# Inverse roots of a local-attention pipeline as exp(-0.5 ln x) under one activation table set, with a Newton step on GpSimd

## The reference

```python
def l2norm(t): return t / jnp.clip(jnp.linalg.norm(t, axis=-1, keepdims=True), 1e-12)

def _layer(x, wqkv, qs, ksc, wo, lg, lb, w1, b1, w2, b2):
    qkv = shift_token(x) @ wqkv                  # 8 heads of 64
    q, k, v = split_into_heads(qkv)
    q = l2norm(q) * qs;  k = l2norm(k) * ksc     # 16 norms a token
    q, k = rotary_xpos(q, k)
    x = x + local_attention(q, k, v) @ wo        # windows of 64, softmax
    h = shift_token(x)
    h = (h - h.mean(-1)) / jnp.sqrt(h.var(-1) + 1e-5) * lg + lb   # 1 norm a token
    a, g = jnp.split(h @ w1 + b1, 2, axis=-1)
    return x + (a * gelu(g)) @ w2 + b2
for l in range(2):
    x = _layer(x, ...)
```

## Time and profile before

| | |
|---|---|
| time, median of 3 runs | 1845.13 us (1841.08 to 1846.48) |
| the profiled execution | 1845.41 us, span 1843.6 us |
| local pipeline, from its first instruction to the tail's | about 1269 to 1656 us of the span |
| busy over the span: PE, DVE, ACT, POOL | 1734.1, 1442.4, 1408.9, 1431.1 us |
| mean granted TensorE clock | 0.976 of full speed |

### The profile page before, as it was taken

One profiled execution on the slowest core, in us unless ns is written; L12 is line 12 of the kernel. 1 busy time (PEld: TensorE's weight loads), 2 busy tenths in 40 slices (PEclk: granted clock), 3 DMA queues, 4 the chain that ended last, 5 costly groups with the idle time before them and its releaser, 6 DMA issues. The chain is left out here.

```text
span 1843.6 us, 54099 instructions
## 1 busy us (share of the span) xinstructions
PE 1734.1 (94%) x22920; PEld 1099.5 (60%) x22920; DVE 1442.4 (78%) x2658; ACT 1408.9 (76%) x1737; POOL 1431.1 (78%) x851
## 2 busy tenths in 40 slices
PE   5999999999999999999999999987899999978997
PEld 2466666666666666666666666675566666653454
DVE  5888888888888888888888887535888888855785
ACT  2688888888888888888888888943898888853464
POOL 6699999999999999999999999974765566634122
PEclk9899999999999999999999999998999999989999
DMA  5101010101011010101010100041111111100000
GB/s 141 27 20 31 19 31 22 28 25 29 24 27 26 25 31 19 31 23 28 23 31 19 28 20 9 2 157 29 40 41 37 37 37 37 33 25 2 1 0 23
DMA packets 71080, 57.02 MB, mean 31 GB/s; under 512 B 29196, under 2 KB 64184, under 8 KB 70840
## 3 DMA queue, kind: packets, MB, share of 16 engines
q1 hardware_dynamic: 70840, 53.57, 11.5%
HBM read 14.67 MB, written 1.05 MB: 9 GB/s over the span
## 5 line engine op out<-in xcount | busy, mean ns | idle before, releaser
L278 POOL TENSOR_TENSOR ah_probs_lo<-ah_probs,ah_probs_hi 128x1024 f16<-128x1024 f32 x512 | 1073.2, 2134 | 78.0 <-ACT ah_probs L487 77.9
L542 DVE TENSOR_REDUCE ah_part_max<-ah_p_m 128x1 f32<-128x512 f32 x1024 | 668.5, 685 | 121.5 <-PE ah_p_m L342 111.2
L484 ACT ACTIVATE ah_probs_hi<-ah_p_s 128x1024 f16<-128x1024 f32 x512 | 530.9, 1037 | 189.6 <-PE ah_p_s L358 178.4
L487 ACT ACTIVATE ah_probs<-ah_p_s 128x1024 f32<-128x1024 f32 x512 | 531.3, 1038 | 0.0
L372 PE MATMUL ah_p_o<-ah_v_hi,ah_probs_hi 128*128 128x65 f16 x4096 | 470.6, 195 | 5.7 <-POOL ah_probs_lo L278 5.1
L374 PE MATMUL ah_p_o<-ah_v_lo,ah_probs_hi 128*128 128x64 f16 x4096 | 470.6, 193 | 0.0
L376 PE MATMUL ah_p_o<-ah_v_hi,ah_probs_lo 128*128 128x65 f16 x4096 | 470.3, 194 | 0.0
L372 PEld LDWEIGHTS ah_p_o<-ah_v_hi,ah_probs_hi 128*128 128x128 f16 x4096 | 383.0, 98 | 84.4 <-DVE a_attn L565 12.2
L374 PEld LDWEIGHTS ah_p_o<-ah_v_lo,ah_probs_hi 128*128 128x128 f16 x4096 | 378.5, 98 | 91.3
L342 PE MATMUL ah_p_m<-ah_k_hi_lo,ah_q_hi_twice 128*128 128x512 f16 x1024 | 393.8, 385 | 6.6 <-DVE ah_part_max L542 3.5
L357 PE MATMUL ah_p_s<-ah_q_hi_twice,ah_k_hi_lo 128*128 128x512 f16 x1024 | 388.6, 380 | 0.8 <-ACT ah_probs L487 0.4
(11 more groups left out here) (316 smaller groups left out, 3083.4 us busy)
## 6 DMA issues: line engine op xcount, KB each, us to landing
ba_v_skew<-ba_v_own SPq DMA_DIRECT2D x64, 129.0 KB, 2.3
ah_q_hi_twice<-ah_hi SPq DMA_DIRECT2D x128, 64.0 KB, 2.0
ah_k_hi_lo<-ah_hi SPq DMA_DIRECT2D x64, 64.0 KB, 1.9
ah_one_k_hi<-ah_hi SPq DMA_DIRECT2D x64, 64.0 KB, 2.0
ah_k_hi_lo<-ah_lo SPq DMA_DIRECT2D x64, 64.0 KB, 2.0
ah_max_q_lo<-ah_lo SPq DMA_DIRECT2D x64, 64.0 KB, 2.0
ah_w_head<-in_w_heads SPq DMA_DIRECT2D x16, 160.0 KB, 2.5
bw_rot<-in_rot SPq DMA_DIRECT2D x4, 512.0 KB, 10.6
```

The lines of the kernel that those rows point to most:

```text
L278: pool.tensor_tensor(pl[:, p % RW, :, :], pb[:, p % RP, :, :], ph[:, p % RW, :, :], ALU.subtract).then_inc(lo_pool, 1)
L484: act.activation(ph[:, p % RW, :, :], p_s[:, p % 2, :, :], ACT.Exp, scale=HD ** -0.5)
L487: act.activation(pb[:, p % RP, :, :], p_s[:, p % 2, :, :], ACT.Exp, scale=HD ** -0.5).then_inc(exp_done, 1)
L542: dve.tensor_reduce(part[:, t, 2 * half + b:2 * half + b + 1], p_m[:, b, :], AX, ALU.max).then_inc(maxed, 1)
```

## The change

The 17 inverse roots of a step are made as exp(-0.5 ln x), and then refined by one Newton step, y(1.5 - 0.5 x y y), in four small POOL instructions. ACT's Sqrt and DVE's reciprocal go. Ln and Exp are both in the set `natural_log_exp_and_others`, which is asked for once at the pipeline's start, once behind each group's Gelu, and once behind `gelu_late`; the softmax's Exp is served by it too. The Newton step stands in POOL's list behind the low part of the probabilities (L1047) and ahead of the product of q and k (L1055). The waits on the square root become waits on the finished inverse root.

```diff
+LOG_AND_EXP = "natural_log_exp_and_others"
...
-        std = sc.sb("root", [P, 2 * HEADS_B + 1])
+        log = sc.sb("log", [P, 2 * HEADS_B + 1])
+        guess = sc.sb("inv_root", [P, 2 * HEADS_B + 1])
+        fix = sc.sb("newton", [P, 3, 2 * HEADS_B + 1])
...
                         if j >= 1:
-                            pool.wait_ge(std_done, j)
+                            pool.wait_ge(rooted, j)
                         pool.tensor_scalar(ssqc[:, :], ssq[:, j % 2, :], 1e-24, None, ALU.max).then_inc(clamped, 1)
...
+                    if on(j) or on(j - 5):
+                        pool.wait_ge(guess_done, j + 1)
+                        pool.tensor_tensor(fix[:, 0, :], guess[:, :], guess[:, :], ALU.mult).then_inc(newton, 1)
+                        pool.wait_ge(newton, 3 * j + 1)
+                        pool.tensor_tensor(fix[:, 1, :], fix[:, 0, :], ssqc[:, :], ALU.mult).then_inc(newton, 1)
+                        pool.wait_ge(newton, 3 * j + 2)
+                        pool.tensor_scalar(fix[:, 2, :], fix[:, 1, :], -0.5, 1.5, ALU.mult, ALU.add).then_inc(newton, 1)
+                        pool.wait_ge(newton, 3 * j + 3)
+                        if on(j - 2):
+                            pool.wait_ge(roped, j - 1)
+                        if on(j - 7):
+                            pool.wait_ge(h2n_done, j - 6)
+                        pool.tensor_tensor(rinv[:, j % 2, :], guess[:, :], fix[:, 2, :], ALU.mult).then_inc(rooted, 1)
...  (ACT: end of gelu_late, then ahead of the loop)
+                    act.preload_act_table_set(LOG_AND_EXP)
+
+                act.preload_act_table_set(LOG_AND_EXP)
                 for j in range(-2, STEPS_B):
...
-                        act.activation(std[:, :], ssqc[:, :], ACT.Sqrt).then_inc(std_done, 1)
+                        act.activation(log[:, :], ssqc[:, :], ACT.Ln).then_inc(log_done, 1)
+                        act.wait_ge(log_done, j + 1)
+                        act.activation(guess[:, :], log[:, :], ACT.Exp, scale=-0.5).then_inc(guess_done, 1)
...
                         act.activation(g_sb[0:LASTN, HC - 1, :], g_sb[0:LASTN, HC - 1, :],
                                        ACT.Gelu).then_inc(gelu_done, 1)
+                        act.preload_act_table_set(LOG_AND_EXP)
...
-                    if on(j) or on(j - 5):
-                        dve.wait_ge(std_done, j + 1)
-                        if on(j - 2):
-                            dve.wait_ge(roped, j - 1)
-                        if on(j - 7):
-                            dve.wait_ge(h2n_done, j - 6)
-                        dve.reciprocal(rinv[:, j % 2, :], std[:, :]).then_inc(rooted, 1)
```

More of the change, by code:

```diff
@@ L943, in local_layers @@
         (consts, cleared, hT_turned, hTh_done, hTl_done, q_ready, k_ready, squared,
-         rq_done, rk_done, ssq_done, clamped, std_done, rooted, nshift_done, t3_done, roped, k_turned, q_turned, khi_done, kxh_done, qhi_done,
+         rq_done, rk_done, ssq_done, clamped, log_done, guess_done, newton, rooted, nshift_done, t3_done, roped, k_turned, q_turned, khi_done, kxh_done, qhi_done,
          klo_done, kxl_done, qlo_done, v_ready, vh_done, vl_done, s_ready, max_done, st_ready, exp_done,
@@ L949, in local_layers @@
              "consts", "cleared", "hT_turned", "hTh_done", "hTl_done", "q_ready", "k_ready",
-             "squared", "rq_done", "rk_done", "ssq_done", "clamped", "std_done", "rooted", "nshift_done", "t3_done", "roped", "k_turned",
+             "squared", "rq_done", "rk_done", "ssq_done", "clamped", "log_done", "guess_done", "newton", "rooted", "nshift_done", "t3_done", "roped", "k_turned",
              "q_turned", "khi_done", "kxh_done", "qhi_done", "klo_done", "kxl_done", "qlo_done", "v_ready",
```

## The result

The changed kernel takes 1852.67 us (median of 7 runs, 1850.12 to 1853.54), the kernel before 1846.36 (7 runs, 1841.08 to 1848.03). The ratio over all runs is 1.0037, with a 95% interval of 1.0027 to 1.0048 (the two medians alone give 1.0034): slower by 0.4%. Forecast were 1846 us and a range that ended at 1851; the profiled execution took 1851.7 us, 6.3 more than that of before. One run of experiment 7, 2496.36 us at a granted clock of 0.65, is left out of its numbers.

What follows compares the result with a forecast made beforehand. PE, ACT and DVE were taken as nearly full, PE's work hiding the loads except in gate steps. Terms -1.5 - 2.4 + 5.4 - 0.7 = +0.8 on 1845.41 gave 1846.2 us; range 1838 to 1851.

Steps and rivals of the forecast that it cites:

- The rival: Half clock behind gate steps, from longer PE idling: 2.7 us over four more groups, 1848.9 us, still no change; chance 0.16.
- the sum's own upper bound: All terms of the forecast at their slow bounds: +7.1 us on the profiled execution.
- The gate steps: Steps with a gate, six times: net +0.90 us each, +5.4 us in all (bounds 0.77 and 1.41 each).
- The load's price: Gate steps: the common set's load between Gelu and the squares makes the squares start 1.41 us later.
- The gain beside it: Gate steps: without the root's load the second gate copy is earlier, so PE's third gate piece gains 0.51 us.
- The drain: Gate steps, by a skill page: squares 1.38 us later still, 8.3 us in six, 1854.5 us in place of 1846.2.
- The steps without a gate: Both loads go but PE hides them: 0.25 us gained per group of four steps, -1.5 us in six groups.
- The steps ahead of the first group: Steps 2 to 9: reciprocal gone and key cast earlier, 0.3 us each, -2.4 us (bounds -1.4 and -5.0).
- First and last steps: Pipeline's ends: in the last steps the residual no longer stands behind root and reciprocal, -0.7 us (bounds 0 and -1.5).
- Newton: Four POOL instructions in each of 37 steps, 1.3 us a step, covered by POOL's idle 2.03 us: cost 0.

Runs made afterwards that it cites:

- experiment 7: The changed kernel with Gelu's load, both Gelus and the load after them moved behind the next step's squares: 1840.43 us, ratio to before 0.9985.
- experiment 2: The kernel before with one added load of the exponential's table set right behind each of the loop's six Gelus: 1858.76 us, ratio 1.0069.
- 4: The changed kernel without its Newton step, the exponential writing the inverse root directly: 1854.66 us, ratio to before 1.0048.
- experiment 3: The changed kernel with a second table load (the exponential's own set) ahead of the load behind each of six Gelus: 1857.93 us, ratio to before 1.0071.
- 8: The changed kernel with Gelu behind the next step's squares, exponentials and v; common-set load ahead of the log: 1837.31 us, or right behind Gelu: 1851.43.
- experiment 1: The changed kernel with the table load that follows each Gelu moved behind the next step's two squares: 1837.12 us, ratio to before 0.9957.

## Why the prediction was wrong

**The step that failed is that of the clock.** The sum left it out of the gate steps: "Nothing gives this back: from there DVE goes to the next step's products in 11.27 us ..." The rival priced it at 4 x 0.68 = 2.7 us, from a mild case in the earlier trace rows, and called it no change; the range, cut at 1851, stopped short even of the sum's own upper bound (1845.41 + 7.1 = 1852.5). Measured, the five steps behind the gate steps took 62.05 and 62.12 us instead of 57.76 and 56.96: +4.7 in the mean, up to 1.85 in one step. With the load behind the squares the same five take 57.47 and 57.39, so it is the load's place that brings it on. How much is not fixed: with the same pause the five took 60.61 us in experiment 2 and 59.10 in 4, with a longer one 59.25 in 3. The traces show what the amount goes by. In the ten executions of all kernels but those of experiments 7 and 8, the granted clock fell to 0.50 behind 27 of 28 pauses of 2.5 us or more, and behind 8 of 22 pauses of 1.11 us, each time for about 3.4 or about 6.8 us:

| half clock in the step behind | steps (long, short pause) | length of that step, us |
|---|---|---|
| none | 1, 14 | 11.24 to 11.28 |
| 3.4 us, from the start of the transposes of q and k (within 0.4 us) | 10, 0 | 11.24 to 11.28 |
| 3.4 us, from 1.6 to 2.4 us after it | 6, 8 | 11.71 to 12.03 |
| 6.8 us, from 0.4 to 1.5 us after it | 11, 0 | 12.72 to 13.18 |

The rival's 0.68 us is a step of the third row; the fourth, which no gate step of the kernel before had shown, was missing. What fixes length and start in a given execution stays open.

**The gate steps** were forecast at 6 x 0.90 = +5.4 and came to +3.7 (87.5 against 83.8). The load's price was right: +1.41 forecast, +1.42 in experiment 2, +1.43 between experiment 1 and the changed kernel. The gain beside it was undersized: the changed kernel without that load is at 13.15 us, 0.72 under before and not 0.51 (in the first of the six, the longest before, 1.22 under). In the step of the earlier trace rows PE had idled not only the 0.51 us for the gate's copy but 0.18 us for DVE's attention rows, and the changed kernel shows neither:

```profile
1418.51 0.66 PE L1187 MATMUL ba_p_o<-g_ident,ba_attn 128*128 128x128 f32 x4 [0.18 <-DVE ba_attn L1448]
```

The waits came as told for DVE (5.25 for 5.2); PE's was 2.53, not 2.0: it grew by the load's whole price, 1.42, where only the net 0.90 was expected.

**The drain.** The Trainium skill, ScalarE: Activation LUTs, section What ACT_TABLE_LOAD costs, adds a drain of about 1380 ns to each switch. It doesn't show here: in experiment 3 a second load added 1.29 to 1.37 us to a gate step, little more than its own 1.283.

**The steps without a gate**: -1.5 forecast, -1.5 measured (119.0 to 117.5, with steps 8 and 9 counted here); PE was full as read, its turned scores still 9.5 us apart. **The steps ahead of the first group**: -2.4 forecast; up to step 8 the gain was 4.2 and 2.0 us in the two executions. The size is right, the reason only in part. The five steps from 1320.65 to 1367.44 went from 9.36 to 9.24 us, a gain of 0.12 and not 0.3 each; most of the rest lies in the first steps, where an execution may meet the half clock or not. **First and last steps**: -0.6 measured at the end, -0.7 forecast, in part by luck: in the changed kernel half clock came in there too (granted 0.78 from 1619 to 1625 us, where before had 1.00 from 1609 to 1621), and with the load behind the squares the same stretch took 45.8 us, -1.3. **Newton** cost nothing, as forecast. DVE lost the reciprocals' 9.4 us, but its busy time fell by only 2.8 us in the first pair of profiles and 6.8 in the second: the reciprocals had overlapped the residuals, and DVE's shift ahead of the pipeline (g_ln_shift, in no edit) took from 1.7 to 4.4 us in these four executions.

With the measured sizes the sum is -1.5 - 3.1 + 3.7 - 0.6 + 4.7 = +3.2 us. The medians differ by 6.3. The two profiled executions of before took 1845.41 and 1849.73, those of after 1851.7 and 1851.59, so these four differ by 4.1 in the mean: the 3.2, and 0.9 in the tail, which both kernels show in one execution or another. The other 2 us are within what single executions of before wander (1841 to 1848), and aren't located.

## What to carry to other kernels

When one table set replaces two, look where the remaining switch goes: a load asked for early stands in its engine's queue ahead of everything behind it, and "early" is only free if what is behind it isn't awaited. Here moving one load behind two instructions turned +0.4% into -0.4%. A pause on TensorE is to be priced with the clock that may follow: count the stall, then the next step at the lower level, less what a wait in it takes up, as a range and not as the mildest case in the trace. And cut a profile at fixed instructions before comparing it: stretches that no edit touches wandered by as much as the effect.

## What the runs showed of the hardware

Not expected was how closely the half clock repeats once two executions fall into step: the changed kernel's two started the pipeline 2.44 us apart, the earlier one met 10.14 us in place of 8.41 in step 2, and from step 8 (1346.47 and 1346.24 us) to the tail they agree within 0.1 us in each of the table's stretches. The two of before reached step 8 1.95 us apart, and behind the first gate step one took 11.96 us and the other 11.24. The kernel without Newton has the same waits on PE but reached step 8 at 1350.71 us, and its half clocks had other lengths and starts. So in these runs the loss behind a gate step looks neither like chance nor like a fixed price of the pause: it goes by how long the half clock lasts and where in the step it falls; what fixes these two wasn't found.
